# Chunked recurrence of a two-layer network: 32-row TensorE tiles, a moved product and two unread products a step

## The reference

```python
def step(S, inp):
    qi, ki, vi, ei = inp
    kh = jnp.einsum('bchd,bhde->bche', ki, S)
    target = vi - ki
    mu = jnp.mean(kh, -1, keepdims=True)
    rstd = jax.lax.rsqrt(jnp.var(kh, -1, keepdims=True) + EPS)
    kh_hat = (kh - mu) * rstd
    g = w * kh_hat + b - target
    gw = g * w
    v_new = (gw - jnp.mean(gw, -1, keepdims=True) - kh_hat * jnp.mean(gw * kh_hat, -1, keepdims=True)) * rstd
    A = jnp.einsum('bchd,bshd->bhcs', qi, ki)
    A = jnp.where(tri, A, 0.0) * jnp.transpose(ei, (0, 2, 1))[:, :, None, :]
    qh = jnp.einsum('bchd,bhde->bche', qi, S) - jnp.einsum('bhcs,bshe->bche', A, v_new)
    o = qi + _ln(qh, w, b)
    S = S - jnp.einsum('bchd,bche->bhde', ki * ei[..., None], v_new)
    return (S, o)
```

## Time and profile before

| what | value |
|---|---|
| three runs, median | 2700.03 us (2691.61 to 2712.86) |
| profiled execution | 2717.68 us, its span 2715.9 us |
| TensorE busy over the span | 2276.5 us, 84% |
| VectorE, ACT, GpSimd busy | 1591.6, 1073.6, 1032.8 us |
| mean granted TensorE clock | 0.892 |
| the chunked recurrence | from about 891 to 1276 us |

### The profile page before, as it was taken

The page is one execution under the profiler, slowest core; times in us unless marked ns, Lnnn a source line. Parts: engine busy times, 40 slices in busy tenths (PEclk is TensorE's granted clock), DMA queues, the critical chain, the costliest instruction groups (busy, mean ns, idle before and its releaser), DMA issues. The chain is left out here.

```text
span 2715.9 us, 50355 instructions
## 1 busy us (share of the span) xinstructions
PE 2276.5 (84%) x19076; PEld 1967.0 (72%) x19076; DVE 1591.6 (59%) x3469; ACT 1073.6 (40%) x2039; POOL 1032.8 (38%) x809
## 2 busy tenths in 40 slices
PE   8999993789887599996669995999999999999930
PEld 6888882667665488885446773899999899999930
DVE  4555554444453386866985642656665566655657
ACT  3222222345554132322442111555555555555523
POOL 3454451121221100001530276656666666656621
PEclk9999996798897696877899997999999999999965
DMA  2110102144433654552431001233344624233147
GB/s 105 36 36 24 36 28 101 68 160 163 157 147 143 184 155 106 157 104 81 155 122 70 1 1 55 84 135 108 107 143 164 215 89 140 80 129 135 40 174 274
DMA packets 154518, 299.74 MB, mean 110 GB/s; under 512 B 66841, under 2 KB 93209, under 8 KB 139645
## 3 DMA queue, kind: packets, MB, share of 16 engines
q1 hardware_dynamic: 108285, 181.82, 20.8%
q0 software_dynamic: 44480, 115.41, 12.6%
q10 hardware_dynamic: 1616, 0.62, 0.1%
HBM read 296.83 MB, written 106.27 MB: 148 GB/s over the span
## 5 line engine op out<-in xcount | busy, mean ns | idle before, releaser
L91 PE MATMUL bank<-routed_xh,routed_guh 128*128 128x256 f32 (+1 forms) x1536 | 438.0, 285 | 27.8 <-DVE routed_xl L2130 27.8
L92 PE MATMUL bank<-routed_xh,routed_gul 128*128 128x256 f32 (+1 forms) x1536 | 437.9, 285 | 0.0
L93 PE MATMUL bank<-routed_xl,routed_guh 128*128 128x256 f32 (+1 forms) x1536 | 435.9, 284 | 0.0
L2164 DVE TENSOR_TENSOR routed_gul<-routed_guf,routed_guh 128x2816 fp32r<-128x2816 f32 x64 | 198.0, 3093 | 250.8 <-ACT routed_guh L2107 250.8
L91 PEld LDWEIGHTS bank<-routed_xh,routed_guh 128*128 128x128 f32 (+1 forms) x1536 | 281.4, 183 | 35.4 <-issue 32.9
L2048 POOL DMA_INDIRECT routed_x<-mid_x,routed_xi x132 | 277.5, 2102 | 55.1 <-issue 52.6
L93 PEld LDWEIGHTS bank<-routed_xl,routed_guh 128*128 128x128 f32 (+1 forms) x1536 | 282.7, 184 | 0.0
L92 PEld LDWEIGHTS bank<-routed_xh,routed_gul 128*128 128x128 f32 (+1 forms) x1536 | 280.8, 183 | 2.1
L2057 POOL DMA_INDIRECT mid_y<-routed_y,routed_yi x132 | 138.8, 1052 | 246.5 <-ACT routed_y L2123 223.9
L2107 ACT CAST routed_guh<-routed_guf 128x2816 fp32r<-128x2816 f32 x64 | 163.5, 2554 | 34.2 <-DMA routed_guf<-in_GU,routed_wi 29.6
L2117 ACT CAST routed_ih<-routed_sil 128x256 fp32r<-128x256 f32 (+1 forms) x192 | 78.0, 406 | 241.4 <-DVE routed_sil L2169 241.4
(11 more groups left out here) (455 smaller groups left out, 5999.5 us busy)
## 6 DMA issues: line engine op xcount, KB each, us to landing
last_y<-mid_y SPq DMA_DIRECT2D x16, 1536.0 KB, 9.7
...
```

The source lines that it names most:

```text
L91: pe.matmul(out, hi(c), whi(c), start=start and c == 0, stop=False, skip_group_check=True)
L92: pe.matmul(out, lo(c), whi(c), start=False, stop=False, skip_group_check=True)
L93: last = pe.matmul(out, hi(c), wlo(c), start=False, stop=stop and c == n - 1, skip_group_check=True)
L2164: nc.vector.tensor_tensor(gul[q][:].rearrange("p a c n -> p (a c n)"), guf[q][:], guh[q][:].bitcast(F32).rearrange("p a c n -> p (a c n)") ...
```

## The change

All of it is in `ttt_recurrence` and in one constant.

- On TensorE the products of a step with 64-row or 128-row weights that hold zeros for other heads are cut into quarters: a batch and a pair of heads each, 32 rows. `cross` times `u`, `am` times `u` and the state update take 32 rows of weights, the products of keys take 64 rows and 32 columns. The state in PSUM lies in two banks, one for each batch; `ub` and `seq` are gone, `S` is stored by batch, and `tri`, `am` and `cross` have half the columns.
- `queries_times_state` stands behind the state update, no longer ahead of the wait for `u`. In its old place stand `FILL` = 2 products of 128 rows and 256 columns into a spare bank, which nobody reads.
- VectorE's two sums become one reduction over `squares`, the two scalings become one product over `pair`; ACT copies `kh` into `pair` first, then squares. `re` is made by GpSimd.
- ACT copies `S` in two halves.

```diff
-    bS, bQ, bA, bC = bank[0:4]
-    bH = bank[4:6]
-    G = KC
-    R64 = HG * TTT
-    tri, seq = ph.sb("tri", [P, R64]), ph.sb("seq", [P, 2])
+    bS, (bQ, bA, bC), bH, spare = bank[0:2], bank[2:5], bank[5:7], bank[7]
+    G, FILL = KC, 2
+    R64, R32, NP = HG * TTT, HG * TTT // 2, 2
+    tri = ph.sb("tri", [P, R32])
...
-    S = ph.sb("S", [P, G, B, DH])
-    am, cross = ph.sb("am", [P, G, R64]), ph.sb("cross", [P, G, R64])
-    u, ub = ph.sb("u", [P, G, DH]), ph.sb("ub", [P, G, B, DH])
-    c1, c2, c3, c4, c5, c6 = (ph.sb(f"c{k}", [P, G, DH]) for k in range(6))
-    eps, m, re = ph.sb("eps", [P, 1]), ph.sb("m", [P, 6, G]), ph.sb("re", [P, G])
+    S = ph.sb("S", [P, B, G, DH])
+    am, cross = ph.sb("am", [P, G, R32]), ph.sb("cross", [P, G, R32])
+    u = ph.sb("u", [P, G, DH])
+    squares, pair, scaled = (ph.sb(n, [P, 2, G, DH]) for n in ("squares", "pair", "scaled"))
+    c1, c2, c3, c4 = (ph.sb(f"c{k}", [P, G, DH]) for k in range(4))
...
             nc.gpsimd.memset(zero[:], 0.0).then_inc(s["zero"], 1)
             nc.gpsimd.memset(kk[0][:], 0.0).then_inc(cleared[0], 1)
             nc.gpsimd.memset(kk[1][:], 0.0).then_inc(cleared[1], 1)
+            for n in range(STEPS):
+                f, r = place(n)
+                pool.wait_ge(s["rs"], n + 1)
+                if r == 0:
+                    pool.wait_ge(in_te[f], 16 * 16 * (n // (2 * ST) + 1))
+                if n:
+                    pool.wait_ge(s["u"], n)
+                nc.gpsimd.tensor_tensor(re[:], m[:, 3], te[f][:, r, :, DH], ALU.mult).then_inc(s["re"], 1)
...
                 if n:
-                    act.wait_ge(s["r2"], n)
-                nc.scalar.activation(c2[:].rearrange("p g e -> p (g e)"), bH[n % 2][:, 0:P], ACT.Square).then_inc(s["sq"], 1)
-                act.wait_ge(s["s2"], n + 1)
-                nc.scalar.activation(m[:, 2], m[:, 1], ACT.Sqrt, scale=1.0 / DH, bias=eps[:, 0:1]).then_inc(s["sd"], 1)
+                    act.wait_ge(s["t"], n)
+                nc.scalar.copy(pair[:, 1].rearrange("p g e -> p (g e)"), bH[n % 2][:, 0:P]).then_inc(s["kh"], 1)
+                nc.scalar.activation(squares[:, 0].rearrange("p g e -> p (g e)"), bH[n % 2][:, 0:P], ACT.Square).then_inc(s["sq"], 1)
+                act.wait_ge(s["sums"], n + 1)
+                nc.scalar.activation(m[:, 2], m[:, 0], ACT.Sqrt, scale=1.0 / DH, bias=eps[:, 0:1]).then_inc(s["sd"], 1)
 
...
-                    act.wait_ge(s["s0"], 1)
-                nc.scalar.copy(S[:].rearrange("p g b e -> p (g b e)"), bS[:, 0:2 * P]).then_inc(s["S"], 1)
+                    act.wait_ge(s["s0"], B)
+                for b in range(B):
+                    last = nc.scalar.copy(S[:, b].rearrange("p g e -> p (g e)"), bS[b][:, 0:P])
+                last.then_inc(s["S"], 1)
...
-                kh = bH[n % 2][:, 0:P].rearrange("p (g e) -> p g e", g=G)
+                dve.wait_ge(s["kh"], n + 1)
+                nc.vector.tensor_tensor(squares[:, 1], pair[:, 1], w2[:], ALU.mult).then_inc(s["xw"], 1)
+                dve.wait_ge(s["xw"], n + 1)
                 dve.wait_ge(s["sq"], n + 1)
-                nc.vector.tensor_reduce(m[:, 1], c2[:], AX, ALU.add).then_inc(s["s2"], 1)
-                nc.vector.tensor_tensor(c3[:], kh, w2[:], ALU.mult).then_inc(s["xw"], 1)
-                dve.wait_ge(s["xw"], n + 1)
-                nc.vector.tensor_reduce(m[:, 4], c3[:], AX, ALU.add).then_inc(s["r1"], 1)
-                dve.wait_ge(s["r1"], n + 1)
-                nc.vector.scalar_tensor_tensor(c4[:], over_e(m[:, 4]), -1.0 / DH, c3[:], ALU.mult, ALU.add).then_inc(s["v1"], 1)
+                nc.vector.tensor_reduce(m[:, 0:2].rearrange("p k g -> p (k g)"), squares[:].rearrange("p k g e -> p (k g) e"), AX, ALU.add).then_inc(s["sums"], 1)
+                dve.wait_ge(s["sums"], n + 1)
+                nc.vector.scalar_tensor_tensor(pair[:, 0], over_e(m[:, 1]), -1.0 / DH, squares[:, 1], ALU.mult, ALU.add).then_inc(s["v1"], 1)
                 dve.wait_ge(s["sd"], n + 1)
+                if n:
+                    dve.wait_ge(s["re"], n)
                 nc.vector.reciprocal(m[:, 3], m[:, 2]).then_inc(s["rs"], 1)
                 dve.wait_ge(s["v1"], n + 1)
                 dve.wait_ge(s["rs"], n + 1)
-                nc.vector.tensor_tensor(c3[:], c4[:], over_e(m[:, 3]), ALU.mult).then_inc(s["t"], 1)
-                nc.vector.tensor_tensor(c1[:], kh, over_e(m[:, 3]), ALU.mult).then_inc(s["hat"], 1)
+                nc.vector.tensor_tensor(scaled[:], pair[:], m[:, 3].unsqueeze(1).unsqueeze(3).to_broadcast([P, 2, G, DH]), ALU.mult).then_inc(s["t"], 1)
                 if r == 0:
                     dve.wait_ge(in_te[f], 16 * 16 * (n // (2 * ST) + 1))
                 dve.wait_ge(s["t"], n + 1)
-                nc.vector.tensor_tensor(c3[:], c3[:], te[f][:, r, :, 0:DH], ALU.add).then_inc(s["gw"], 1)
-                nc.vector.tensor_tensor(re[:], m[:, 3], te[f][:, r, :, DH], ALU.mult).then_inc(s["re"], 1)
-                dve.wait_ge(s["hat"], n + 1)
+                nc.vector.tensor_tensor(c1[:], scaled[:, 0], te[f][:, r, :, 0:DH], ALU.add).then_inc(s["gw"], 1)
                 dve.wait_ge(s["gw"], n + 1)
-                nc.vector.tensor_tensor(c2[:], c3[:], c1[:], ALU.mult).then_inc(s["p"], 1)
+                nc.vector.tensor_tensor(c2[:], c1[:], scaled[:, 1], ALU.mult).then_inc(s["p"], 1)
...
-                nc.vector.tensor_tensor(u[:], c6[:], over_e(re[:]), ALU.mult).then_inc(s["u"], 1)
-                dve.wait_ge(s["u"], n + 1)
-                if n + 1 < STEPS:
-                    nc.vector.tensor_tensor(ub[:], u[:].unsqueeze(2).to_broadcast([P, G, B, DH]),
-                                            seq[:].unsqueeze(1).unsqueeze(3).to_broadcast([P, G, B, DH]), ALU.mult).then_inc(s["ub"], 1)
+                nc.vector.tensor_tensor(u[:], c4[:], over_e(re[:]), ALU.mult).then_inc(s["u"], 1)
                 dve.wait_ge(s["A"], n + 1)
-                nc.vector.tensor_tensor(am[:], bA[:, 0:G * R64].rearrange("p (g n) -> p g n", g=G),
-                                        tri[:].unsqueeze(1).to_broadcast([P, G, R64]), ALU.mult).then_inc(s["am"], 1)
+                nc.vector.tensor_tensor(am[:], bA[:, 0:G * R32].rearrange("p (g n) -> p g n", g=G),
+                                        tri[:].unsqueeze(1).to_broadcast([P, G, R32]), ALU.mult).then_inc(s["am"], 1)
...
+            def quarters():
+                for b in range(B):
+                    for p in range(NP):
+                        yield b, p, slice((b * NP + p) * R32, (b * NP + p + 1) * R32)
+
             def keys_times(out, n, other, made):
                 for g in range(G):
-                    for b in range(B):
-                        last = pe.matmul(out[half(b), g * R64:(g + 1) * R64], keys(n, g, b), other(g, b),
+                    for b, p, q in quarters():
+                        feats, toks = slice(p * NP * DH, (p + 1) * NP * DH), slice(p * R32, (p + 1) * R32)
+                        last = pe.matmul(out[q, g * R32:(g + 1) * R32], keys(n, g, b)[feats, toks], other(g, b)[feats, toks],
                                          start=True, stop=True, skip_group_check=True)
...
-            pe.matmul(bS[:, 0:2 * P], zero[:, 0:P], zero[:], start=True, stop=False, skip_group_check=True).then_inc(s["s0"], 1)
+            for b in range(B):
+                pe.matmul(bS[b][:, 0:P], zero[:], zero[:], start=True, stop=False, skip_group_check=True).then_inc(s["s0"], 1)
...
                 f, r = place(n)
                 pe.wait_ge(s["S"], n + 1)
                 if n + 1 < STEPS:
                     keys_times_state(n + 1).then_inc(s["KS"], 1)
-                if n:
-                    pe.wait_ge(s["qh"], n)
-                queries_times_state(n)
+                for _ in range(FILL):
+                    pe.matmul(spare[:, 0:G * R64], KQ[f][:, 0, 0, r, 0:2].rearrange("p g t -> p (g t)"), KQ[f][:, 0, 1, r].rearrange("p g t -> p (g t)"),
+                              start=True, stop=True, skip_group_check=True)
                 pe.wait_ge(s["u"], n + 1)
                 if n + 1 < STEPS:
                     pe.wait_ge(s["cross"], n + 1)
                     for g in range(G):
-                        for b in range(B):
-                            last = pe.matmul(bH[(n + 1) % 2][half(b), g * DH:(g + 1) * DH], cross[half(b), g, :], u[half(b), g, :],
+                        for b, p, q in quarters():
+                            last = pe.matmul(bH[(n + 1) % 2][q, g * DH:(g + 1) * DH], cross[q, g, :], u[q, g, :],
                                              start=False, stop=True, skip_group_check=True)
                     last.then_inc(s["KH"], 1)
-                    pe.wait_ge(s["ub"], n + 1)
                     for g in range(G):
-                        last = pe.matmul(bS[:, g * B * DH:(g + 1) * B * DH], kk[f][:, r, g].rearrange("p j d -> p (j d)"),
-                                         ub[:, g].rearrange("p b e -> p (b e)"), start=False, stop=False, skip_group_check=True)
```

(14 more changed lines are left out.)

25 lines of the change are left out of this document (13 added, 12 removed).

## The result

The changed kernel takes 2825.4 us (median of 4 runs, 2811.3 to 2833.8) against 2695.8 us for the kernel before run beside it (4 runs): ratio 1.044, 95% interval 1.040 to 1.049. It is slower by 4.4%, where 2658 us was forecast. Its profiled execution took 2824.4 us.

A forecast was written before the change was run, and what follows sets the result against it. Bound: TensorE at the low clock (7.44 us a step), the ACT-VectorE-TensorE loop at the full (4.87). Two steps at 7.44 and 61 at 4.78 make 306.5 instead of 348.1 us: 41.6 off the 2700.0 median gives 2658, range 2636 to 2704.

The forecast's parts named there:

- VectorE and ACT: Path from ACT's start to TensorE's load of `u`: 4.28 us against 4.18, a loss of 0.10 us a step.
- TensorE's pairs: TensorE's load and matmul pairs, 104 to 196 a step: sum 3.90 us against 4.16, `cross` on the loop 0.20 shorter.
- what a pair costs decides: Pricing of TensorE's small-tile pairs: bounds 0.008 and 0.030 us each; the lower was taken, time going with columns.
- The queries' product moved: Queries' product behind the state update: ACT's copies of `S` end near 2.0 us, TensorE needs them about 2.1; nothing late.
- The transfers: SyncE's load issues per eight-step tile: 12 us free, shorter steps take 6 of them.
- The clock, the main term: TensorE in the recurrence: dense unread products hold 2.4 GHz after the first steps; of 41.6 us gained, all but 5.5.
- Rival B: TensorE's pairs come no faster than 0.030 us, so a step takes 6.9 us: slower, 2786 us; chance 0.15.

The follow-up runs named there:

- e8: Kernel before with only the change's VectorE, ScalarE and GpSimd edits, TensorE's products as before: 2743.1 us, ratio 1.013.
- e5: Kernel before with 46 unread products of 32x32 tiles added in each step, 196 pairs as in the changed kernel: 2828.7 us, ratio 1.044.
- e11: Kernel before with only the queries' product moved behind the state update, nothing filling its old place: 2757.2 us, ratio 1.018.
- e4: Changed kernel without the data loads from the third eight-step tile on (output not the reference's): 2771.8 us, ratio 1.024 to the kernel before.
- e13: e9 without the data loads from the third eight-step tile on (output not the reference's): 2671.8 us, ratio 0.987 to the kernel before.
- e9: Kernel before with one unread product a step and `cross` times `u` in 32x32 tiles, 122 pairs a step: 2726.5 us, ratio 1.009.
- e3: Kernel before with only two unread products a step added ahead of the wait for `u`: 2706.5 us, ratio 1.000.
- e6: Changed kernel with three unread products and half the quarter products left out, 118 pairs (output not the reference's): 2705.4 us, ratio 0.999 to before.

## Why the prediction was wrong

- **VectorE and ACT: right.** +0.10 us forecast, +0.07 measured (4.94 against 4.87 in e8). The reduction over 256 columns takes 0.42, the scaling 0.45, GpSimd's `re` 0.20, hidden. What was missed is that these edits also cost clock: e8 is 37 us slower, where 0.07 us in each of 63 steps is 4, and its low share is 0.45 against 0.35. That the longer wait brings the clock down is argued from this alone.
- **TensorE's pairs: right in price, wrong in what it left out.** `cross` 0.34 (forecast 0.34), the masked product 0.34 (0.34), keys 0.61 for 61 (0.60 for 64), the state update 0.56 (0.55), the two unread products 1.06 (0.97). The sum was right for a TensorE that has its instructions. The step "what a pair costs decides" failed: it priced a pair's time on the engine and not its supply, a term that the sum doesn't have. What the runs showed in its place is a stop wherever a block of 128 pairs came late: 24 in the changed kernel, 30 in e5, which has only the pairs.
- **The Trainium skill** (TensorE: Matmul & The Clock Gate, Wait — 56ns, not 53.3ns?) has a floor of about 25 ns between matmul starts. The trace does not agree for matmuls on different tiles: 32 pairs in 0.34 us are 11 ns each, on four tiles side by side.
- **The queries' product moved: right at the full clock** (e11's floor is 4.87), but without the filling it is dear: e11 is 1.8% slower, by the clock, for a reason that stays open.
- **The transfers: wrong.** They land in time, but their packets delay the instructions: e4 is 54 us faster than the changed kernel, e13 55 us faster than e9.
- **The clock, the main term: wrong.** "I expect that the clock then stays at 2.4 GHz" came true where the pairs were few: e3 has 0.98, e13 1.00. With 24 stops it was 0.60, and the low clock cost some 119 us where curing it was to give 36. Whether the changed kernel would hold the clock with instructions at hand isn't shown: no run has its 196 pairs without stops, and e6, with its order and 118 pairs, still was low for 0.24. The prediction drew on a stretch of before in which the clock came back while TensorE worked without a wait; in the changed kernel it stayed low for seven steps without a stop (994 to 1044 us). At the low clock TensorE is the bound, and the unread products, 2.08 us a step, stand on its path.
- **Rival B** gave 2786 us and was nearest (2825), but for another reason, so that its nearness is luck. No pair is slow; blocks of 128 pairs come too late. The period at which it decides, 5.53 us, is 0.028 us for each of 196 pairs; the runs with 192 to 198 pairs had means of 0.033 to 0.037. It got a chance of 0.15 on rows of 32 loads each (1 us), too short a stretch to see a block run out.
